# Splitting a top-k selection 18 and 14 instead of 20 and 12, and moving its rounds to other periods

## The reference

```python
x = layernorm(x + attn_block(x))     # RWKV: three projections k, v, r, two scans over
                                     # the tokens, a gate, an output projection
# second block, on the x made above
weights = (x @ router_w)[..., 0] + router_b[0]
k = int(0.125 * s)                   # 64 of the 512 tokens
topv, topi = top_k(weights, k); thr = topv[:, -1]
sel_idx = sort(topi[:, :k - 1])      # 63 tokens of each sequence, in order
# on the 63 tokens: rms norm, 16-head attention with RoPE and a mask, MLP with gelu
out = zeros_like(x).at[bidx, sel_idx].set((x_sel + attention + mlp) * w_sel)
out = out + x * (1 - (weights > thr))
x = layernorm(x + out)
```

## Time and profile before

| | |
|---|---|
| median of 3 runs | 769.72 us (769.6 to 769.82) |
| profiled execution | 775.65 us |
| its span, first to last instruction | 773.9 us |
| PE busy | 728.7 us (94%) |
| DVE busy | 648.4 us (84%) |
| ACT busy | 515.7 us (67%) |
| POOL busy | 512.5 us (66%) |
| mean granted PE clock | 0.974 of full speed |

### The profile page before, as it was taken

One profiled execution on the slowest core, in us unless ns is written; L12 is line 12 of the kernel. 1 busy time (PEld: TensorE's weight loads), 2 busy tenths in 40 slices (PEclk: granted clock), 3 DMA queues, 4 the chain that ended last, 5 costly groups with the idle time before them and its releaser, 6 DMA issues. The chain is left out here.

```text
span 773.9 us, 12972 instructions
## 1 busy us (share of the span) xinstructions
PE 728.7 (94%) x4334; PEld 539.3 (70%) x4334; DVE 648.4 (84%) x1326; ACT 515.7 (67%) x983; POOL 512.5 (66%) x495
## 2 busy tenths in 40 slices
PE   7899999999999999999988899988999998999993
PEld 5466666666666666676555676767787776899993
DVE  6798998989989899999999998787977677567784
ACT  3568888888888888888866674775656766632120
POOL 1687887878878778787667667855548773631333
PEclk9999999999999999999999999997999999999997
DMA  8012424233242332422322201234001120000001
GB/s 235 4 52 63 144 69 136 68 100 103 68 134 71 91 114 69 123 81 68 104 88 82 68 29 48 90 103 130 16 15 56 43 82 2 2 7 23 28 17 39
DMA packets 37336, 55.38 MB, mean 72 GB/s; under 512 B 3360, under 2 KB 26528, under 8 KB 37280
## 3 DMA queue, kind: packets, MB, share of 16 engines
q1 hardware_dynamic: 34464, 46.28, 19.6%
q0 software_dynamic: 2816, 8.39, 3.6%
HBM read 35.78 MB, written 18.87 MB: 71 GB/s over the span
## 5 line engine op out<-in xcount | busy, mean ns | idle before, releaser
L804 PE MATMUL ps<-halves 128*128 128x512 f32 x558 | 238.7, 536 | 0.0
L799 PE MATMUL ps<-arena,wa 128*128 128x512 f32 x384 | 204.5, 615 | 15.5 <-DVE arena L1591 6.9
L804 PEld LDWEIGHTS ps<-halves 128*128 128x128 f32 x558 | 107.5, 193 | 100.1 <-issue 91.6
L819 PE MATMUL ps<-wa,arena 128*128 128x256 f32 x512 | 131.7, 380 | 0.0
L605 POOL TENSOR_TENSOR arena<-arena 128x1024 f32<-128x1024 f32 x32 | 76.3, 2384 | 78.4 <-issue 54.9
L589 POOL TENSOR_TENSOR arena<-arena 128x512 f32<-128x512 f32 x93 | 116.4, 1281 | 5.5 <-ACT halves L1215 5.5
L799 PEld LDWEIGHTS ps<-arena,wa 128*128 128x128 f32 x384 | 71.0, 192 | 45.2 <-POOL halves L590 14.1
L1559 DVE TENSOR_TENSOR_SCAN arena<-ewb,ps 128x511 f32<-128x511 f32 x64 | 74.5, 1205 | 27.8 <-ACT ps L1187 26.9
L819 PEld LDWEIGHTS ps<-wa,arena 128*128 128x128 f32 x512 | 87.3, 190 | 6.6
L596 POOL TENSOR_TENSOR arena<-arena 128x1024 f32<-128x1024 f32 x32 | 76.2, 2380 | 22.5 <-ACT arena L1201 22.5
L1586 DVE TENSOR_TENSOR_SCAN arena<-ewb,ps 128x511 f32<-128x511 f32 x64 | 74.1, 1199 | 0.0
(11 more groups left out here) (233 smaller groups left out, 1511.0 us busy)
## 6 DMA issues: line engine op xcount, KB each, us to landing
arena<-x_chan SPq DMA_DIRECT2D x32, 512.0 KB, 4.2
out<-arena SPq DMA_DIRECT2D x32, 512.0 KB, 3.3
arena<-x_chan SPq DMA_DIRECT2D x64, 127.8 KB, 3.3
wa<-w_attn SPq DMA_DIRECT2D x1, 1024.0 KB, 7.2
wa<-w_up SPq DMA_DIRECT2D x1, 1024.0 KB, 6.1
wa<-w_down SPq DMA_DIRECT2D x1, 1024.0 KB, 5.5
wqk<-w_qk SPq DMA_DIRECT2D x1, 512.0 KB, 5.0
wv<-w_v SPq DMA_DIRECT2D x1, 256.0 KB, 5.2
```

Of the source, the lines that this page charges most:

```text
L799: mm(bank[:, o, :], wa[:, m, 0, out_part], xm[s.par][:, m, :], start=True, stop=False)
L804: last = mm(bank[:, o, :], w[:, m, out_part], x[s.par], start=False, stop=(t == 2))
L819: last = mm(psY[:, j, :], gg[s.par][:, c, tokens], wa[:, 3, c, :], start=False, stop=(c == CC - 1))
```

## The change

`SEQS` becomes sequences 0 to 17 and 18 to 31 (so pairs 0 to 8 and 9 to 15). Everything of group 0 up to `token_weights` and `token_halves` comes two periods earlier, the eight rounds are laid over six periods (21 to 26) instead of four (23 to 26), and `slots_chosen` and all behind it stay where they are. In the second stage group 1, now of 14 sequences, has its rounds in pairs (two late in 2, one early and two late in 3 and again in 4), so that `slots_chosen` comes late in 4 and early in 5, and `slots_turn`, the one-hots and the picks each come one period earlier; the last batch has four pairs instead of three.

```diff
-    SEQS = ((0, 20), (20, 32))
-    SA = 20
+    SEQS = ((0, 18), (18, 32))
+    SA = 18
@@ POOL: which pairs are gathered in which period
-                if q in (1, 3, 7, 9):
-                    first, past, batch = {1: (4, 7, 2), 3: (7, 10, 3), 7: (10, 13, 4), 9: (13, NP, 5)}[q]
+                if q in (1, 3, 6, 8):
+                    first, past, batch = {1: (4, 7, 2), 3: (7, 9, 3), 6: (9, 12, 4), 8: (12, NP, 5)}[q]
@@ PE: weights_turn(0) at 21 instead of 23; in the second stage
                 if n == 2:
-                    picks(7, 10, 4, PICKED)
+                    picks(7, 9, 4, PICKED)
+                if n == 5:
+                    slots_turn(1, 4, PICKED)
                 if n == 6:
-                    slots_turn(1, 4, PICKED)
+                    picks(9, 12, 4, PICKED)
                 if n == 7:
-                    picks(10, 13, 4, PICKED)
-                if n == 8:
-                    picks(13, NP, 4, PICKED)
+                    picks(12, NP, 4, PICKED)
@@ DVE, first stage
-                if n == 20:
-                    tables_for_pairs()
-                if n == 22:
-                    token_weights(0)
-                if n == 23:
-                    weights_copied(0)
-                    top_round(0, 0)
-                if n == 25:
-                    token_halves(0)
-                if 24 <= n <= 26:
-                    top_round(0, 2 * (n - 24) + 1)
-                    top_round(0, 2 * (n - 24) + 2)
-                if n == 26:
-                    top_round(0, 7)
+                if n == 18:
+                    tables_for_pairs()
+                if n == 20:
+                    token_weights(0)
+                if n == 21:
+                    weights_copied(0)
+                if n == 23:
+                    token_halves(0)
+                if 21 <= n <= 26:
+                    for k in ((0,), (1,), (2,), (3, 4), (5,), (6, 7))[n - 21]:
+                        top_round(0, k)
@@ DVE, second stage, selection_early
                 if n == 3:
-                    top_round(1, 1)
+                    top_round(1, 2)
                 if n == 4:
-                    top_round(1, 4)
+                    top_round(1, 5)
                 if n == 5:
-                    top_round(1, 7)
-                if n == 6:
                     slots_chosen(1, 1)
@@ DVE, second stage, selection_late
                 if n == 1:
-                    for q in range(7, 10):
+                    for q in range(7, 9):
                         one_hot(q)
                 if n == 2:
                     weights_copied(1)
                     top_round(1, 0)
+                    top_round(1, 1)
                 if n == 3:
-                    top_round(1, 2)
                     top_round(1, 3)
+                    top_round(1, 4)
                     token_halves(1)
                 if n == 4:
-                    top_round(1, 5)
                     top_round(1, 6)
+                    top_round(1, 7)
+                    slots_chosen(1, 0)
                 if n == 5:
-                    slots_chosen(1, 0)
+                    slots_copied_of(1, 4, PICKED)
+                    for q in range(9, 12):
+                        one_hot(q)
                 if n == 6:
-                    slots_copied_of(1, 4, PICKED)
-                    for q in range(10, 13):
+                    keep_values(9, 12, 4, PICKED, 4)
+                    for q in range(12, NP):
                         one_hot(q)
                 if n == 7:
-                    keep_values(10, 13, 4, PICKED, 4)
-                    for q in range(13, NP):
-                        one_hot(q)
-                if n == 8:
-                    keep_values(13, NP, 4, PICKED, 5)
+                    keep_values(12, NP, 4, PICKED, 5)
```

More of the change, by code:

```diff
@@ L454, in group_of @@
         def group_of(q):
-            return 0 if q < 10 else 1
+            return 0 if q < 9 else 1
         def tables_of(first):
@@ L868, in selection @@
             def selection(n):
-                if n in (23, 29, 30):
+                if n in (21, 29, 30):
                     pe.wait_ge(clamp_done, n + 1)
-                if n == 23:
+                if n == 21:
                     weights_turn(0)
@@ L880, in selection_read @@
             def selection_read(n):
-                if n >= 24:
+                if n >= 22:
                     pe.wait_ge(w_copied, 1)
@@ L1045, in selection_b_read @@
                     pe.wait_ge(values_kept, 3)
+                if n == 6:
+                    pe.wait_ge(slots_copied, 2)
                 if n == 7:
-                    pe.wait_ge(slots_copied, 2)
+                    pe.wait_ge(values_kept, 4)
                 if n == 8:
-                    pe.wait_ge(values_kept, 4)
-                if n == 9:
                     pe.wait_ge(values_kept, 5)
@@ L1289, in period @@
                     rows_of(at.back(3))
-                if isinstance(at.n, int) and at.n == 23:
+                if isinstance(at.n, int) and at.n == 21:
                     rms_of(0)
@@ L1850, in selection_late @@
                     token_weights(1)
-                    for q in range(7, 10):
+                    for q in range(7, 9):
                         one_hot(q)
                 if n == 2:
-                    keep_values(7, 10, 4, PICKED, 3)
+                    keep_values(7, 9, 4, PICKED, 3)
                     weights_copied(1)
                     top_round(1, 0)
+                    top_round(1, 1)
                 if n == 3:
-                    top_round(1, 2)
                     top_round(1, 3)
+                    top_round(1, 4)
                     token_halves(1)
                 if n == 4:
-                    top_round(1, 5)
                     top_round(1, 6)
+                    top_round(1, 7)
+                    slots_chosen(1, 0)
                 if n == 5:
-                    slots_chosen(1, 0)
+                    slots_copied_of(1, 4, PICKED)
+                    for q in range(9, 12):
+                        one_hot(q)
                 if n == 6:
-                    slots_copied_of(1, 4, PICKED)
-                    for q in range(10, 13):
+                    keep_values(9, 12, 4, PICKED, 4)
+                    for q in range(12, NP):
                         one_hot(q)
                 if n == 7:
-                    keep_values(10, 13, 4, PICKED, 4)
-                    for q in range(13, NP):
-                        one_hot(q)
-                if n == 8:
-                    keep_values(13, NP, 4, PICKED, 5)
+                    keep_values(12, NP, 4, PICKED, 5)
                 if n == 12:
```

## The result

| | before | after |
|---|---|---|
| median | 770.12 us (766.74 to 774.26, 9 runs) | 774.98 us (769.81 to 780.16, 9 runs) |
| ratio after to before | | 1.0061, 95% interval 1.0036 to 1.0086 |
| profiled execution | 775.65 us | 777.15 us |
| its span | 773.9 us | 775.4 us |
| its mean granted PE clock | 0.974 | 0.969 |

The change makes the kernel 0.61% slower, some 4.7 us. The forecast was 768.9 us, 0.8 under before, with 771.6 as its upper end: it was wrong in its sign.

What follows compares the result with a forecast made beforehand. PE sets the pace early in the first stage, DVE from 374 us on through the selection. Terms: -2.4 + 0.2 + 1.4 = -0.8 us, so 769.72 - 0.8 = 768.9 us; range 765.9 to 771.6.

Steps and rivals of the forecast that it cites:

- First stage, -2.4 us: Periods 20 and 21: DVE, then the bound, has 1.21 us free of selection in each; gain 2 x 1.21 = 2.4 us.
- Periods 2 to 4 at nothing: Second stage: the extra late round in period 2 costs nothing, as DVE's wait in period 3 covers it; uncovered 0.9 us.
- DVE's wait of 1.81 us in period 3: Second stage: DVE waits 1.81 us for PE's values, said to cover the 1.49 less 0.6 us put back in period 2.
- Loss 0.2 us: Second stage, periods 5 to 8: 46.6 us after against 46.4 before, a loss of 0.2 us with PE at full clock.
- 46.6 us: Second stage, forecast sum of periods 5 to 8 at full clock: 14.0 + 11.0 + 11.8 + 9.8 us.
- The size of the terms: Second stage at full clock: period 5 14.0 us, 6 11.0, 7 11.8 with rope 7 0.3 late, 8 9.8.
- The clock, 1.4 us: Second stage, period 5: a low PE clock expected with 3.7 us of waits, costing 0.8 to 1.7, taken as 1.4.
- Rival B: Second stage, periods 4 and 5: DVE's chain holds PE 3.7 us, low clock follows; 2.8 us slower, 772.5; chance 0.14.
- Its point of decision: Second stage: Rival B decides from a loss there of 2.4 + 1.5 = 3.9 us.
- Rival A: Clock does not fall in period 5, or spares another stretch: -2.2 us, 767.5, or 765.8 with one spared; chance 0.35.
- The rule of HAM oscillation: PE: matmul groups with waits between them each start slow; by it the second stage loses 3.3 us to the clock.

Runs made afterwards that it cites:

- first_only: Kernel before with only the first stage's new schedule, for sequences 0 to 17; sequences 18 and 19 not selected, constant router weights: 767.77 us, ratio 0.9974 to before.
- filled pair: Kernel before and changed kernel, both with extra unread matmuls in PE's waits of the second stage, on one chip: 770.47 and 772.30 us.
- before_warm2: Kernel before plus unread matmuls: five each in PE's waits of periods 4 and 6, eight each ahead of `o_turn` in periods 3 and 4: 770.47 us, ratio 0.9960.
- second_only: Kernel before with only the second stage's new order, groups still 20 and 12: 777.91 us, ratio 1.0092 to before.
- warm: Changed kernel plus twelve and five unread matmuls in PE's two waits of period 5: 768.14 us, ratio 0.9986 to before.
- the chip of the last experiments: Chip where the filled pair, the changed kernel again (775.99 us, ratio 1.0062) and the kernel before (772.72 us) ran, 12 runs each.
- rounds_early: Changed kernel with one of the second group's rounds moved from period 4 to period 2: 780.33 us, ratio 1.0054 to before.
- two_rounds_out: Changed kernel with the second group's last two rounds (6 and 7) left out, so its last 16 places are not selected: 775.37 us, ratio 0.9995 to before.
- warm_late: Changed kernel with `slots_turn` of period 5 moved behind `project_o` and twelve unread matmuls ahead of that period's mask pick: 772.84 us, ratio 0.9968 to before.
- after_warm2: Changed kernel plus unread matmuls: twelve and five in period 5's waits, eight each ahead of `o_turn` in periods 3 and 4: 772.30 us, ratio 0.9992 to before.

## Why the prediction was wrong

1. **First stage, -2.4 us: right in mechanism and size, with a part lost behind it.** Up to period 29 the gain is 2.64 us, and `first_only` as a whole is 2.0 us faster. In both profiled pairs 1.6 us of it goes in period 30, which takes 19.29 us instead of 17.65, because PE's low clock behind the picks lasted longer there (0.50 over 465 to 470, before 0.72). This is not the rule: of the nine profiles with the new first stage three have 19.3 us in period 30 and six 17.65, and of the four with the old one three have 17.65 and one 20.92.
2. **Periods 2 to 4 at nothing: right in the sum, not in the reason.** They take 34.92 against 35.14 us in the filled pair. The forecast let DVE's wait of 1.81 us in period 3 cover the earlier round. That wait stood behind a mask pick and values that a low clock had stretched to 1.88 and 2.57 us; in `before_warm2` and `first_only`, where the values take 1.85, DVE has no such wait. Without the cover the new order costs 1.46 us: periods 2 to 4 take 34.45 us in `second_only` and 32.99 in `first_only`, both at full clock. The whole change has 33.38 in `warm`, as period 2 picks one pair fewer (10.91 us instead of 11.86). In the first pair of profiles the changed kernel was even 2.8 us faster here (36.56 against 39.40). 2.1 of that lie in period 2, where before has a wait that the changed kernel's profile lacks (last section), and 1.2 in period 4, where before waits 0.96 us ahead of the mask pick and the changed kernel does not. Neither is shown to be the change's doing, and both hide part of the 4.2 us lost behind them.
3. **Periods 5 to 8 at full clock, "Loss 0.2 us": this step failed.** It compared unlike sums. The forecast's 46.6 us were at full clock, and the 46.4 of before held a low stretch of 1.7 that the prediction itself names. At full clock before is 9.78 + 11.80 + 11.04 + 12.12 = 44.74 us (`before_warm2`), so the forecast's own terms already said a loss of 1.9 where it wrote 0.2. The 1.4 that was then added for the clock only brought the changed kernel up to the one stretch before had in that place: it charged no additional clock to the change at all.
4. **The size of the terms.** Period 5 was 14.52 for 14.0 and period 7 12.56 for 11.8: there a wait of 0.44 us ahead of the mask pick and one of 0.18 for POOL came in, where 0.3 was counted in all. Period 8 was 9.78 in the profile of the change, as forecast, but 11.33 on the chip of the last experiments (its wait is shown in the last section). With 1.9 for the sum above this gives 1.9 + 0.5 + 0.8 = 3.2 us at full clock, and 4.7 where period 8 is longer.
5. **The clock, 1.4 us: by these estimates the larger part of the miss.** It was priced as one stretch in one place. In the first comparison, mean clocks of 0.973 and (from the 29 runs of before) 0.980 at 6 us for each 0.01 make about 4.3 of the 4.7 us lost; on the chip of the last experiments, 0.975 and 0.979 make about 2. Taken the other way, by difference, 4.7 lost and 2.4 gained in the first stage less the 3.2 at full clock leave 3.9 us for it. Both are estimates; that low clock behind the waits costs time is shown by the fillers, how much more of it the change has is not. The price in period 5 of the profile is 2.7 us (17.25 less 14.53), against 1.7 behind the one wait of 1.05 before and the 1.4 charged.
6. **Rival B happened.** It named this chain, a hold of 3.7 us and low stretches behind it, and said 772.5; it got 0.14. Its point of decision, a loss of 3.9 us in the second stage, was passed: 50.6 - 46.4 = 4.2 in the profile. Of its low stretches the profile has the long one in period 5 (2.7 us for 3.3) and none in period 6 or 7, and the result lies 2.5 us above its 772.5. The chance was too small because the 1.9 of point 3 was missing from the middle of the forecast. Rival A's argument, that the places of the low clock are drawn anew, is true of single executions, but on average more waits brought more low clock: 0.973 for the changed kernel and `second_only`, 0.972 for `rounds_early`, 0.983 where the waits of period 5 were filled.
7. **The rule of HAM oscillation** in the Trainium skill (TensorE: Matmul & The Clock Gate) says that matmul groups with waits between them each start slow; the prediction took it as agreeing only in part and did not use it. For period 5 the runs are nearer to it than the value taken: in all six profiles of the new order without a filler the waits there were followed by a low clock, a single one of 1.05 us (`two_rounds_out`) among them, and keeping PE at work through them took it away. Elsewhere they agree only in part: waits of 1.35 us (`warm_late`) and 1.76 us (`first_only`) were not followed by one.

## What to carry to other kernels

Before two sums of periods are subtracted, bring both to the same clock: take out of the kernel before what its low stretches cost, then charge the clock to both by the waits that each has. Look, too, whether a wait that is to cover something stands in a low stretch: at full clock it may not be there. Here a wait on the engine that sets the pace cost its length, and often 1.7 to 2.7 us more through the clock behind it; two short waits instead of one long one gained nothing. Where such a wait can't be removed, matmuls whose result nobody reads can fill it: here ten to seventeen of them gave 0.45 to 0.75%, and the fastest complete kernels of this study are the one before with fillers (0.9955 and 0.9960), not a version of the change (0.9968 at best, with intervals that overlap).

## What the runs showed of the hardware that was not expected

**A low clock without a wait.** In the changed kernel PE is busy 4.71 of 5 us over 460 to 465, with 0.29 us as its only wait, at the beginning, in the narrow matmuls of the picks (16 to 48 columns). Right behind them it runs at 1.2 GHz: L799 takes 2.06 us for two where it takes 1.02 else.

```profile
464.46 0.62 PE L861 MATMUL ps<-halves 128*128 128x48 f32 x4
464.91 1.01 PE L865 MATMUL ps<-halves 128*128 128x32 f32 x4
465.76 2.06 PE L799 MATMUL ps<-arena,wa 128*128 128x512 f32 x2
```

So not every low stretch stands behind a wait. All profiles of this study have a low stretch behind these picks, between 460 and 475 us. A filler has no place in it, and none was tried.

**DVE and ACT can stand still together.** In `after_warm2` both engines wait in period 8 for something that the trace calls remote, without naming an engine:

```profile
589.49 0.60 ACT L1390 ACTIVATE arena<-ps 128x512 f32<-128x512 f32 x1 [1.01 <-remote]
590.95 0.69 DVE L1821 TENSOR_TENSOR arena<-ps,trg 128x512 f32<-128x512 f32 x1 [3.13 <-remote]
```

PE's scores then wait 1.72 us, and period 8 is 11.33 instead of 9.78. All seven profiles of the second and third chip have such waits between 560 and 600 us, the four of the first chip and that of the changed kernel none. The profile of the kernel before has them too (2.89 us on DVE at 585.15), but PE waits only 0.63 us in that period, which takes 12.1 us with them and without (`first_only`). The same eight profiles, and no others, have such a wait in period 2 as well, where it costs before some 1.1 us (13.0 for 11.89) and the changed kernel 2.1 (13.05 for 10.91). So the two profiles that the result was read from differ in this, and it is no effect of the change. At a clock of 0.980 the changed kernel is 0.3 us over before in the first comparison and 1.8 on the last chip; the 1.5 us of period 8 are of that size, but that they are the cause is not shown. What is waited for stays open, and so does whether it goes by chip.
